# Two-layer decoder on one core: the rotated-heads stage written with small product tiles, and 36 products ahead of its first rows

## The chip, the core and the metric

The kernel runs on one core of one Trainium2 chip, by itself. The time is the device time of one execution in microseconds (us). In the texts PE is TensorE (matrix products), PEld its weight loads, DVE is VectorE, ACT is ScalarE, POOL is GpSimd and SP is SyncE. The engines run their own instruction lists in order and wait for one another on semaphores. Products write to PSUM, which has eight banks.

## What is computed

A decoder of two layers over 32 batch entries of 100 rows and 256 columns in float32. Each layer adds to the rows an attention, a cross-attention to a context and a feed-forward part with experts. The change touches the attention of layer 1 alone ("the rotated heads"), cut here to what matters:

```python
Q = (x @ wq + bq).reshape(Bn, Sn, Hn, hd)     # 16 heads of 16; K and V alike
def prep(t):                                   # for Q and for K
    h1 = jnp.tanh(jnp.einsum('bshd,do->bsho', t, w1) + b1)
    return jnp.einsum('bsho,on->bshn', h1, w2) + b2
q1 = jnp.einsum('bshn,nm->bshm', qc, Hc)       # qc: prep(Q) as 8 complex numbers
qe = jnp.real(jnp.einsum('hcb,bshn->cshn', R, q1))  # R turns entries 0..7 in pairs, else the identity
qq = jnp.sum(qe ** 2, -1)
kk = jnp.sum(ke ** 2, -1)
s = qq[:, :, None, :] * kk[:, None, :, :]
attn = jax.nn.softmax(s / s, axis=2)
out = jnp.einsum('bijh,bjhd->bihd', attn, V).reshape(Bn, Sn, Dn)
return out @ wo + bo
```

Since s / s is 1, the weights are uniform where s is finite and not zero, so each output row is the mean of V over the entry's rows, times a factor of 1 that is still worked out from the squared sizes of every query and of the largest and smallest key of each head.

## The kernel before

The kernel is a chain of stages (self-attention, cross-attention, a mixture stage, the rotated heads, a wide cross-attention, the experts). Each stage is a block of five instruction lists, one for each engine, and the next block begins when all five have ended. The order within a list is the order of the code; no scheduler changes it.

The stage at issue is `rotation_phase` (line 1916). It takes the 32 entries as 16 pairs (`LANES` = 2 entries, 400 columns together: two chunks of 128 of the 256 features, two entries, 100 rows). The entries of pairs 0 to 3 are the *turned* ones (`TURNED` = 4); for pairs 4 to 15 R is the identity. For each pair PE does

- `make_rows` (L2050): four transposes of the normalised rows into the bank `side`;
- `make_part` (L2057), once for K and once for Q: four products of 200 columns into `side`;
- `first_layer` 0 to 7 (L2084): four products of 32 rows and 400 columns, side by side on four row groups of the array, into two of six banks (`BANK_PAIRS` = 3 pairs of banks in turn); ACT takes each bank pair with one tanh (L2210);
- `last_layer` 0 to 3 (L2098): eight products of 32 output rows and 400 columns, side by side on four column groups, into the bank `vec`;
- `make_mean` (L2065): four products of 2 columns into `side`;
- for a turned pair `mix` (L2106, L2108) for K and for Q: one product of 400 columns and two of 200;
- `norms` (L2113) for K and for Q: one product of 128 by 128 on 400 columns, which writes each head's sum of squares to all 16 rows of the head;
- `project` (L2119): four products of 256 columns.

Step k of PE interleaves pair k with the pair before (its query norms and projection) and the pair after (its rows, K, Q and mean). `side` is one bank that all of these share one after another; each user has to wait until DVE or ACT has read what the one before left. ACT copies rows, K and Q out of it (`keep_rows`, `keep_part`), DVE does the rest: `ends_of_keys` (largest and smallest key), `spans`, `weigh` (a reciprocal and three products over 400 columns), `add` (the projection onto x), and also `combine`, `second_norm`, `stats` and `apply`, which end the mixture stage for the pair after next and normalise its rows; POOL gathers rows for `combine` by indirect DMA and works out the roots, the bias and the second norm's scale.

SP waits until the rows of pairs 0 and 1 are stored and then starts the loads of the next stage's weights.

## Time and profile before

| | us |
|---|---|
| median of 3 runs | 3473.21 (3470.78 to 3478.59) |
| the profiled execution | 3493.37, its span 3491.2 |
| the rotated-heads stage in it, from the first product of its tables to its last add | 1228.6 to 1641.0 |
| first rows of the stage reach PE | 1247.1 |
| last product of the stage before, first product of the stage after | 1223.9, 1647.6 |
| PE busy in the span | 3271.7 (94%) |
| DVE, ACT, POOL busy in the span | 1814.3 (52%), 1613.6 (46%), 1520.3 (44%) |
| mean granted TensorE clock, as a share of 2.4 GHz | 0.97 |

The granted clock is at one of two levels, 1.00 (2.4 GHz) or 0.50 (1.2 GHz). In this stage it stands at 0.50 from the first table product until 1268.0 and again from 1633.6 to 1640.0. A timeline row gives start, duration, engine, line, operation, what is written and read, how many instructions are merged into it, and in brackets how long the engine was idle before it and who ended that. A product in float32 shows as two records, so x8 on PE is four products; transposes show as one. Since records overlap, the cost of a group of products is best read as the time from its start to the start of the next group.

### The profile page before, as it was taken

The numbers are of one execution on the slowest core, as the hardware profiler recorded it, in microseconds if no ns is written. First come the engines' busy times: TensorE is split into PE (matmuls) and PEld (weight loads), VectorE is DVE, ScalarE is ACT, GpSimd is POOL, SyncE is SP. The second block draws the span as 40 slices with busy tenths as digits, with TensorE's granted clock in tenths as the row PEclk, the third lists the DMA queues.
The fourth block names the chain that finished last, engine by engine and source line by source line (L and its number), as shares of the span: only waits on it lengthen the run. The fifth ranks groups of instructions, "written<-read, shape, count | busy, mean of one in ns | idle before, by whom it ended". The sixth has DMA issues, their size and how long they took to land. (4 is left out here: it accounts for less than half of the span.)

```text
span 3491.2 us, 70582 instructions
## 1 busy us (share of the span) xinstructions
PE 3271.7 (94%) x26268; PEld 2383.1 (68%) x26269; DVE 1814.3 (52%) x5671; ACT 1613.6 (46%) x3299; POOL 1520.3 (44%) x2061
## 2 busy tenths in 40 slices
PE   8997999988998869998999999999999999999997
PEld 6774566656776734443677777777777688999986
DVE  4665777755887545664444545454545465111123
ACT  4653666655764046775445554555555411111111
POOL 1002444434775154551566566666666554000035
PEclk9999999998998879999999999999999999999998
DMA  8501111100000630001000000000000013999952
GB/s 279 207 2 42 42 42 42 43 26 1 21 23 25 196 90 20 20 20 38 8 8 14 8 8 8 14 8 8 8 14 1 1 38 129 326 326 325 325 185 78
DMA packets 111486, 263.29 MB, mean 75 GB/s; under 512 B 24003, under 2 KB 70240, under 8 KB 95840
## 3 DMA queue, kind: packets, MB, share of 16 engines
q1 hardware_dynamic: 90208, 224.70, 20.1%
q0 software_dynamic: 16384, 26.29, 2.7%
q10 hardware_dynamic: 4608, 8.39, 0.6%
q8 instruction: 191, 3.13, 0.4%
q14 instruction: 95, 0.78, 0.1%
HBM read 196.61 MB, written 62.65 MB: 74 GB/s over the span
## 5 line engine op out<-in xcount | busy, mean ns | idle before, releaser
L2546 POOL TENSOR_SCALAR wide_probs<-wide_probs,wide_inverse 100x361 f32<-100x361 f32 x512 | 603.9, 1192 | 0.1
L2813 ACT ACTIVATE wide_probs<-wide_probs,wide_least 100x361 f32<-100x361 f32 x512 | 300.9, 592 | 8.6 <-DVE wide_least L2910 8.6
L2910 DVE CUSTOM_DVE_ANT_0 wide_probs<-banks,wide_bias 100x361 f32<-100x361 f32 x512 | 251.6, 529 | 45.1 <-issue 40.0
L2598 PE MATMUL banks<-w_wide_v,wide_c 64*120 64x512 f32 (+1 forms) x1152 | 266.4, 591 | 0.9 <-DVE wide_v L2896 0.9
L2592 PE MATMUL banks<-wide_c,w_wide_k 64*128 64x361 f32 x1536 | 257.4, 467 | 7.4 <-DMA wide_c<-in_ctxT 7.4
L2210 ACT ACTIVATE rot_h<-banks,w_rot_b 128x800 f32<-128x800 f32 x256 | 223.6, 924 | 86.2 <-PE banks L2084 81.1
L2544 POOL TENSOR_TENSOR wide_hold_pool<-eps 100x1 f32<-100x1 f32 x256 | 49.4, 193 | 455.1 <-DVE wide_inverse L2916 455.1
L3354 ACT ACTIVATE tiles_hT<-banks 128x512 f32<-128x512 f32 x114 | 68.1, 597 | 347.8 <-PE banks L3270 347.8
L3270 PEld LDWEIGHTS banks<-tiles_xT,tiles_w 128*128 128x128 f32 x1824 | 214.1, 193 | 4.5 <-issue 1.6
L2592 PEld LDWEIGHTS banks<-wide_c,w_wide_k 64*128 64x128 f32 x1536 | 150.5, 189 | 96.6 <-issue 10.5
L2625 PE MATMUL banks<-wide_kT,wide_qT 64*100 64x361 f32 x1024 | 208.4, 478 | 8.3 <-DVE wide_least L2910 6.6
L3270 PE MATMUL banks<-tiles_xT,tiles_w 128*128 128x128 f32 x1824 | 214.6, 276 | 1.2 <-DVE tiles_xT L3516 1.2
L3283 PE MATMUL banks<-tiles_w,tiles_hT 128*128 128x256 f32 x912 | 206.4, 379 | 0.3 <-issue 0.3
L3192 POOL TENSOR_TENSOR combine_hold<-eps 100x1 f32<-100x1 f32 x32 | 7.6, 236 | 442.0 <-DMA slots<-tiles_out 431.9
L2598 PEld LDWEIGHTS banks<-w_wide_v,wide_c 64*120 64x120 f32 (+1 forms) x1152 | 120.7, 180 | 107.1 <-issue 93.3
L3283 PEld LDWEIGHTS banks<-tiles_w,tiles_hT 128*128 128x128 f32 x912 | 168.8, 190 | 21.1 <-issue 0.4
L2643 PEld LDWEIGHTS banks<-ident,wide_probs 100*120 100x120 f32 (+1 forms) x1536 | 142.5, 140 | 31.2 <-issue 29.3
L2643 PE MATMUL banks<-ident,wide_probs 100*120 100x100 f32 (+1 forms) x1536 | 158.8, 254 | 3.0 <-ACT wide_probsT L2819 3.0
L2807 ACT COPY wide_v<-banks 120x512 f32<-120x512 f32 (+1 forms) x96 | 56.2, 585 | 223.7 <-PE banks L2598 223.7
L2804 ACT COPY wide_kT<-banks 128x361 f32<-128x361 f32 x128 | 59.0, 461 | 205.7 <-PE banks L2592 205.7
L2920 DVE COPY wide_probsT<-banks 121x400 f32<-121x400 f32 x128 | 72.9, 570 | 151.2 <-PE banks L2643 151.2
L2655 PE MATMUL banks<-wide_probsT,wide_v 120*64 120x100 f32 (+1 forms) x3072 | 148.9, 253 | 0.1
(469 smaller groups left out, 7378.6 us busy)
## 6 DMA issues: line engine op xcount, KB each, us to landing
tiles_w<-in_moe_w SPq DMA_DIRECT2D x114, 1024.0 KB, 5.1
slots<-zeros SPq DMA_DIRECT2D x58, 512.0 KB, 5.7
cross_c<-in_ctxT SPq DMA_DIRECT2D x32, 270.8 KB, 4.4
wide_c<-in_ctxT SPq DMA_DIRECT2D x32, 270.8 KB, 4.0
mix_kT<-slots SPq DMA_DIRECT2D x32, 256.0 KB, 4.2
slots<-mix_m_tiles_out ACTq DMA_DIRECT2D x32, 256.0 KB, 4.0
tiles_rows<-slots SPq DMA_DIRECT2D x57, 128.0 KB, 4.7
slots<-tiles_out SPq DMA_DIRECT2D x57, 128.0 KB, 4.9
```

The source lines that it names most:

```text
L2210: nc.scalar.activation(t.h[:, u % 2, m, 2 * half:2 * half + 2, :], pair_banks(i), ACT.Tanh, bias=w.b1[:, m:m + 1]).then_inc(h_done[i], 1)
L2546: last = nc.gpsimd.tensor_scalar(t.probs[:, i, j, :], t.probs[:, i, j, :], t.inverse[:, i, j:j + 1], None, ALU.mult)
L2592: last = nc.tensor.matmul(make_bank(unit, lane)[:, 0:CTX], w.k[rows_of(lane), k, at:at + P], t.c[rows_of(lane), of.buf, k, :], start=(k == ...
L2598: last = nc.tensor.matmul(make_bank(unit, lane)[0:kw, :], t.c[rows_of(lane), of.buf, k, k0:k0 + kw], w.v[rows_of(lane), k, of.hf * BANK:(o ...
L2625: last = nc.tensor.matmul(scores(j), t.qT[rows_of(j), here.hf, m, lane, :], t.kT[rows_of(j), here.hf, m, lane, :], start=True, stop=True)
L2643: last = nc.tensor.transpose(turned(bank)[0:cols, at], t.probs[:, i, j, k0:k0 + cols], g.ident[0:S, 0:S])
L2655: last = nc.tensor.matmul(out[rows_of(j), :], t.v[0:kw, of.hf, k, LANE_OF(i), at:at + WD], t.probsT[0:kw, group % STEP_GROUPS, bank, cols] ...
L2813: last = nc.scalar.activation(t.probs[:, i, j, :], t.probs[:, i, j, :], ACT.Exp, bias=t.least[:, i, j:j + 1], scale=-1.0, accum_out=t.rows ...
L2910: last = nc.vector.tensor_tensor_reduce(t.probs[:, i, j, :], scores(j), t.bias[:, :], -1.0, LARGEST, ALU.add, ALU.min, t.least[:, i, j:j + 1])
L2920: nc.vector.tensor_copy(t.probsT[:, group % STEP_GROUPS, 0, :], turned(0)[0:TMAX, 0:TURN_COLS]).then_inc(b[group].probsT_dve, 1)
L3270: last = nc.tensor.matmul(out_, t.w1[:, lane, c, m * P:(m + 1) * P], t.xT[:, lane, c, :], start=(c == 0), stop=(c == DC - 1))
L3283: last = nc.tensor.matmul(tile_out, t.hT[:, lane, m, :], t.w2[:, lane, m, :], start=(m == 0), stop=(m == HM - 1))
```

## The change

The stage is written anew. The products that make up the two layers, the rows, K, Q and the mean are the same in number and shape. Others are cut differently:

- `norms` is four products of 32 output rows and 100 columns, one for each entry and chunk, each on its own column group (`COPIES` = 4 copies of each of 8 heads' sums instead of 16). What follows from them on DVE (`ends_of_keys`, `spans`, `weigh`) runs over 128 by 100 instead of 128 by 400.
- `mix` writes 64 output rows for each chunk, so the two chunks use two column groups; the squares of a turned pair are 200 columns instead of 400.
- The projection is two steps: `make_projected` multiplies the mean, masked by head and copied (`masked`, from DVE), with the projection's weights (four products of 32 output rows and 256 columns on four column groups), DVE copies the result (`keep_projected`), and `project` multiplies the factors with it (two products of 64 rows and 256 columns; for pairs 4 to 15 into two banks, `side` and `vec`; for turned pairs into one, the second waiting for the first through `lane_ready`).
- `keep_rows` and `keep_part` move from ACT to DVE, but for pair 0.
- The mean of a pair is made one step later, next to the rows of another; the order of the groups in a step and of DVE's and POOL's work is new. POOL reads the gather's indices directly, without DVE's copy.
- Between the table products and the first rows PE issues `WARM_UPS` = 36 products of 128 by 128 on 400 columns of the loaded weights into the six banks; nothing reads them.
- ACT runs one tanh of a single column ahead of the first rows.
- On DVE at the stage's head `combine` of pair 1 comes ahead of `apply` of pair 0, and the storing of pair 1's rows moves from POOL to DVE.

```diff
+CHUNK_HEADS = P // HD
+COPIES = 4
+GROUP_ROWS = CHUNK_HEADS * COPIES
+MIXED = CHUNK_HEADS * NQ
+LAST_PAIR = PAIRS - 1
+WARM_UPS = 36
...
+        def norms_in(p, part):
+
+            if is_turned(p):
+                return D, lambda lane, c: t.sum_mixed[:, c * GROUP_ROWS:(c + 1) * GROUP_ROWS], lambda lane, c: mixed_lanes(t.squares[:, part, :])[:, lane, :]
+            return 0, lambda lane, c: t.sum8[:, :], lambda lane, c: by_both(t.squares[:, part, :])[:, c, lane, :]
...
-            def norms(pr, part, ready):
-                pe.wait_ge(squares[part], pr[2])
-                nc.tensor.matmul(side[:, 0:COLS], t.sum8[:, :], t.squares[:, part, :], start=True, stop=True).then_inc(ready, 1)
...
-            def project(pr):
-                pe.wait_ge(s.headsT, pr[2])
...
                 for lane in range(LANES):
                     for c in range(DC):
-                        last = nc.tensor.matmul(by_lane(side)[:, lane, :], t.headsT[:, c, lane, :], w.proj[:, c, :], start=(c == 0), stop=(c == DC - 1))
-                last.then_inc(s.proj_ready, 1)
...
+                for c in range(DC):
+                    nc.tensor.matmul(side[c * MIXED:(c + 1) * MIXED, 0:LANES * S], t.real[:, :], by_chunk(t.by_cos)[:, c, :], start=True, stop=False)
...
+                        last = nc.tensor.matmul(mixed_lanes(side)[c * MIXED:(c + 1) * MIXED, lane, :], t.imag[:, :], by_both(t.by_sin)[:, c, 1 - lane, :], start=False, stop=(lane == LANES - 1))
+                last.then_inc(mixed_ready[part], 1)
+
+            def norms(p, part, out, ready):
+                pe.wait_ge(squares[part], p + 1)
+                _, sums, rows = norms_in(p, part)
+                for lane in range(LANES):
+                    for c in range(DC):
+                        group = lane * DC + c
+                        last = nc.tensor.matmul(out[group * GROUP_ROWS:(group + 1) * GROUP_ROWS, :], sums(lane, c), rows(lane, c), start=True, stop=True)
+                last.then_inc(ready, 1)
+
+            def make_projected(p):
+
+                pe.wait_ge(s.masked, p + 1)
+                for group in range(LANES * DC):
+                    last = nc.tensor.matmul(rows_out[group * GROUP_ROWS:(group + 1) * GROUP_ROWS, :], t.masked[:, group, :, :].rearrange("p h r -> p (h r)"), w.proj[:, group % DC, :], start=True, stop=True)
+                last.then_inc(s.rows_ready, 1)
+
+            def project(p):
+                pe.wait_ge(s.ratio, p + 1)
+                pe.wait_ge(s.rows, p + 1)
+                half = P // LANES
+                if two_banks(p):
+                    for lane, out in ((0, side), (1, vec)):
+                        last = nc.tensor.matmul(out[0:S, 0:D], t.least[lane * half:(lane + 1) * half, :], t.rows[lane * half:(lane + 1) * half, :], start=True, stop=True)
+                    last.then_inc(s.proj_ready, 1)
+                else:
+                    nc.tensor.matmul(by_lane(side)[:, 0, :], t.least[0:half, :], t.rows[0:half, :], start=True, stop=True).then_inc(s.lane_ready, 1)
+                    pe.wait_ge(s.lane_ready, p + 1)
+                    nc.tensor.matmul(by_lane(side)[:, 1, :], t.least[half:P, :], t.rows[half:P, :], start=True, stop=True).then_inc(s.proj_ready, 1)
...
+            def step(k):
+                before, after = k - 1, k + 1
+                late = not two_banks(before)
+                first_layer(k, 2)
+                if before >= 0:
+                    if before > 0:
+                        pe.wait_ge(s.added, before * LANES)
+                    pe.wait_ge(s.k_ends, k)
+                    pe.wait_ge(s.q_kept, k + 1)
+                    make_mean(before)
+                    if is_pair(after):
+                        make_rows(after)
+                first_layer(k, 3)
+                last_layer(k, 0)
+                if before >= 0:
+                    if is_pair(after):
+                        pe.wait_ge(s.yT, after + 1)
+                    pe.wait_ge(s.mean, before + 1)
+                    if is_turned(before):
+                        mix(before, 0)
+                    else:
+                        norms(before, 0, query_norms(before), s.qn_ready)
+                first_layer(k, 4)
+                if before >= 0 and is_pair(after):
+                    if is_turned(before):
+                        pe.wait_ge(squares[0], before + 1)
+                    else:
+                        pe.wait_ge(s.spans, before + 1)
...
+                first_layer(k, 5)
+                last_layer(k, 1)
+                if before >= 0:
+                    if is_pair(after):
...
+                    make_projected(before)
+                    if is_turned(before):
+                        norms(before, 0, query_norms(before), s.qn_ready)
+                first_layer(k, 6)
...
+                elif late:
+                    pe.wait_ge(s.rows, before + 1)
+                    pe.wait_ge(s.spans, before + 1)
                     make_part(after, 0, s.q_ready)
...
+                else:
+                    pe.wait_ge(squares[1], k + 1)
+                    project(before)
+                first_layer(k, 7)
+                last_layer(k, 2)
+                if before < 0:
+                    pe.wait_ge(s.k_kept, after + 1)
+                elif late:
+                    pe.wait_ge(s.q_kept, after + 1)
+                else:
+                    pe.wait_ge(s.added, (before + 1) * LANES)
+                if is_turned(k):
+                    mix(k, 1)
+                else:
+                    norms(k, 1, key_norms, s.kn_ready)
...
+                        pe.wait_ge(s.k_ends, k + 1)
+                    if before >= 0 and late:
+                        project(before)
+                    else:
+                        make_part(after, 0, s.q_ready)
+                    first_layer(after, 1)
...
-            make_rows(FIRST)
-            pe.wait_ge(s.yT, 1)
-            make_part(FIRST, 1, s.k_ready)
-            pe.wait_ge(s.k_kept, 1)
-            make_part(FIRST, 0, s.q_ready)
...
+            for k in range(WARM_UPS):
+                nc.tensor.matmul(pair_banks(k)[:, 0, :], w.qkv[:, 0, 0:P], w.qkv[:, 1, 0:COLS], start=True, stop=True)
+            make_rows(0)
+            make_part(0, 1, s.k_ready)
+            first_layer(0, 0)
+            make_part(0, 0, s.q_ready)
+            first_layer(0, 1)
...
+            nc.scalar.activation(t.warm[:, :], w.b1[:, 0:1], ACT.Tanh)
...
-            def keep_rows(pr):
-                act.wait_ge(s.yT_ready, pr[2])
-                nc.scalar.copy(t.yT[:, :, :, :], by_both(side)).then_inc(s.yT, 1)
...
+                    combine(following)
+                if is_pair(after):
+                    keep_rows(after)
+                if before >= 0:
+                    keep_mean(before)
+                if is_pair(after):
+                    add_rows_up(after)
+                if before >= 0 and not is_turned(before):
                     spans(before)
-                if after:
-                    apply(after)
-                if before:
                     weigh(before)
-                if following:
+                if before < 0:
                     combine(following)
-                if after:
-                    add_rows_up(after)
-                if third:
-                    copy_slots(third)
-                if following:
+                    turn_by(k, 1)
```

PE, the last half of a step in the middle of the stage, pairs that are not turned, in the kernel before:

```order
L2084 MATMUL banks<-rot_q,rot_w 128x400 x4
L2119 MATMUL banks<-w_rot_proj,rot_headsT 100x256 x4
L2098 MATMUL banks<-rot_h,rot_w 32x400 x8
L2084 MATMUL banks<-rot_q,rot_w 128x400 x4
L2065 MATMUL banks<-rot_ybar,w_rot_qkv 128x2 x4
L2084 MATMUL banks<-rot_q,rot_w 128x400 x4
L2113 MATMUL banks<-rot_squares,rot_sum 128x400
L2098 MATMUL banks<-rot_h,rot_w 32x400 x8
L2084 MATMUL banks<-rot_q,rot_w 128x400 x4
L2113 MATMUL banks<-rot_squares,rot_sum 128x400
L2084 MATMUL banks<-rot_q,rot_w 128x400 x4
```

The projection and both norms in a step of the changed kernel (L2079 is `first_layer`, L2095 `last_layer`, L2052 `make_part`, L2060 `make_mean`, L2116 `norms`, L2123 `make_projected`, L2132 `project`):

```order
L2116 MATMUL banks<-rot_squares,rot_sum 32x100 x4
L2079 MATMUL banks<-rot_q,rot_w 128x400 x4
L2052 MATMUL banks<-rot_yT,w_rot_qkv 128x200 x4
L2079 MATMUL banks<-rot_q,rot_w 128x400 x4
L2095 MATMUL banks<-rot_h,rot_w 32x400 x8
L2123 MATMUL banks<-w_rot_proj,rot_masked 32x256 x4
L2079 MATMUL banks<-rot_q,rot_w 128x400 x4
L2132 MATMUL banks<-rot_rows,rot_least 100x256 x2
L2079 MATMUL banks<-rot_q,rot_w 128x400 x4
L2095 MATMUL banks<-rot_h,rot_w 32x400 x8
L2116 MATMUL banks<-rot_squares,rot_sum 32x100 x4
```

Two single products of 400 columns have become fours of 100 columns, the projection's four products have become four narrow ones and two; between the two first_layer groups around `project` only that short group is left, where before a last_layer or `make_mean` stood.

PE at the head of the stage in the changed kernel, from the tables to the first layer of pair 0:

```order
L2031 MATMUL banks<-w_rot_hadamard,w_rot_w2T 128x32 x4
L2033 MATMUL banks<-ones,w_rot_v_b 128x1 x2
L2035 MATMUL banks<-w_rot_b,rot_fold_b 128x1
L2228 MATMUL banks<-w_rot_qkv 128x400 x36
L2044 MATMUL banks<-ident,rot_y 128x100 x4
L2052 MATMUL banks<-rot_yT,w_rot_qkv 128x200 x4
L2079 MATMUL banks<-rot_q,rot_w 128x400 x4
L2052 MATMUL banks<-rot_yT,w_rot_qkv 128x200 x4
```

The 36 products stand ahead of the transposes of pair 0 in the same list, so those can't begin before all 36 have been issued.

DVE, one step of the changed kernel from the copy of the rows on:

```order
L2385 COPY rot_yT<-banks 128x400
L2393 SCALAR_TENSOR_TENSOR rot_mean<-banks,rot_v_b 128x2x2
L2397 TENSOR_TENSOR rot_masked<-rot_mean,own_scaled 128x128
L2389 TENSOR_REDUCE rot_ybar<-rot_yT 128x4
L2429 TENSOR_SCALAR rot_least<-banks,rot_k_least 128x100
L2430 TENSOR_SCALAR rot_most<-banks,rot_k_most 128x100
L2436 RECIPROCAL rot_inverse<-rot_least 128x100
L2438 TENSOR_TENSOR rot_least<-rot_least,rot_inverse 128x100
L2440 SCALAR_TENSOR_TENSOR rot_least<-rot_most,rot_least 128x100
L2403 TENSOR_SCALAR rot_q<-banks,w_rot_qk_b 128x200 x2
```

The two copies, of rows and of K, now stand in DVE's list among the short operations of the pair before, right behind `combine` of the pair after next.

## Rows read from the trace of the kernel before

**Rows 1.** Windows of the stage: us, busy per engine (instructions), PE clock, DMA share.

```profile
1233.00:1247.10 14.10, 0.00 (x0) 0.00 (x0) 7.53 (x27) 0.00 (x0) 9.11 (x16) 0.50 0.18 50
1247.10:1268.10 21.00, 17.28 (x72) 10.12 (x76) 7.14 (x21) 10.24 (x14) 13.62 (x22) 0.50 0.49 142
...
1286.70:1367.50 80.80, 73.90 (x544) 36.12 (x540) 46.94 (x110) 49.87 (x69) 38.87 (x66) 1.00 0.06 16
1367.50:1392.20 24.70, 23.07 (x182) 11.07 (x178) 14.62 (x36) 16.71 (x23) 11.44 (x21) 1.00 0.04 10
1392.20:1611.40 219.20, 214.40 (x1683) 100.33 (x1680) 131.89 (x306) 168.23 (x230) 117.45 (x202) 1.00 0.07 18
1611.40:1629.00 17.60, 15.15 (x128) 5.47 (x124) 7.24 (x10) 11.55 (x14) 0.00 (x0) 1.00 0.00 1
1629.00:1641.00 12.00, 4.65 (x14) 2.44 (x10) 6.18 (x8) 0.59 (x1) 0.00 (x0) 0.72 0.00 0
1647.60:1653.60 6.00, 5.99 (x20) 3.83 (x22) 1.34 (x2) 0.46 (x1) 1.77 (x3) 0.50 1.05 368
```

**Rows 2.** Timeline of PE, one step of pairs that are not turned.

```profile
1440.39 0.53 PE L2050 MATMUL banks<-ident,rot_y 100*128 100x100 f32 x4
...
1441.73 1.62 PE L2057 MATMUL banks<-rot_yT,w_rot_qkv 128*128 128x200 f32 x8
...
1448.09 0.95 PE L2084 MATMUL banks<-rot_q,rot_w 32*128 32x400 f32 x8
1449.07 1.97 PE L2119 MATMUL banks<-w_rot_proj,rot_headsT 128*100 128x256 f32 x8
1450.97 1.55 PE L2098 MATMUL banks<-rot_h,rot_w 128*32 128x400 f32 x16
1452.45 0.95 PE L2084 MATMUL banks<-rot_q,rot_w 32*128 32x400 f32 x8
1453.34 1.05 PE L2065 MATMUL banks<-rot_ybar,w_rot_qkv 128*128 128x2 f32 x8
1454.52 0.95 PE L2084 MATMUL banks<-rot_q,rot_w 32*128 32x400 f32 x8
1455.40 0.94 PE L2113 MATMUL banks<-rot_squares,rot_sum 128*128 128x400 f32 x2
1456.27 1.55 PE L2098 MATMUL banks<-rot_h,rot_w 128*32 128x400 f32 x16
```

**Rows 3.** Timeline of PE, the mixes and the norms of a turned pair.

```profile
1362.87 0.94 PE L2106 MATMUL banks<-rot_by_cos,rot_real 128*128 128x400 f32 x2
1363.65 0.84 PE L2108 MATMUL banks<-rot_by_sin,rot_imag 128*128 128x200 f32 x4
1365.16 0.94 PE L2113 MATMUL banks<-rot_squares,rot_sum 128*128 128x400 f32 x2 [0.67 <-ACT rot_squares L2215]
...
1369.34 0.91 PE L2106 MATMUL banks<-rot_by_cos,rot_real 128*128 128x400 f32 x2 [0.88 <-DVE rot_by_sin L2337]
```

**Rows 4.** Timeline of PE, the mixture stage: narrow products of 100 columns, side by side.

```profile
901.06 0.88 PE L750 MATMUL banks<-mix_probsT,mix_v 100*17 100x100 f32 x32
```

**Rows 5.** Timeline of PE, the expert stage: a dense stream of products of 256 columns.

```profile
2959.77 3.62 PE L3283 MATMUL banks<-tiles_w,tiles_hT 128*128 128x256 f32 x16
2963.22 3.73 PE L3270 MATMUL banks<-tiles_xT,tiles_w 128*128 128x128 f32 x32
```

**Rows 6.** Timeline of PE, step 15: a first_layer group that waits for the tanh.

```profile
1617.92 0.95 PE L2084 MATMUL banks<-rot_q,rot_w 32*128 32x400 f32 x8 [1.11 <-ACT rot_h L2210]
```

**Rows 7.** Timeline of DVE: combine of one pair until its next work, and the last reciprocal.

```profile
1444.55 0.87 DVE L2304 SCALAR_TENSOR_TENSOR rot_moe_sum<-rot_moe_got,mix_coef,mix_x 100x256 f32<-100x256 f32 x2
...
1447.20 0.54 DVE L2325 TENSOR_REDUCE rot_ybar<-rot_yT 128x4 f32<-128x400 f32 x1
...
1631.88 2.65 DVE L2357 RECIPROCAL rot_inverse<-rot_least 128x400 f32<-128x400 f32 x1
```

556 lines of the change are left out of this document (277 added, 279 removed).

## The prediction

> **What bounds the kernel now.** I read the page first: PE is busy for 94% of the span, and the stages follow one another without overlap, so the stage that is changed can be costed alone. Its windows [rows 1] say the same of the stage. Between 1392.2 and 1611.4, which is steps 5 to 14 (pairs that are not turned), PE is busy for 214.4 of 219.2 us, ACT for 168, DVE for 132: PE is the bound, at 21.92 us a step. Steps 1 to 3 (1286.7 to 1367.5) take 26.93 us each, step 4 24.7, step 15 17.6. The tail after the last last_layer takes 12.0. At the head PE does nothing from 1233 to 1247.1; then it works at half clock for 21 us, and step 0 ends at 1286.7, 39.6 us after the first rows.
>
> **What a product costs.** Eight products of 256 columns take 3.45 us from start to start [rows 5], 1.69 ns a column, so 400 columns are 0.675. The lone norms group takes 0.87, first_layer (four side by side) 0.88, last_layer (two rounds of four) 1.48 against 1.35 [rows 2]: a group costs its columns plus 0.13 to 0.2 us. Four products on four column groups cost one. This holds for narrow short ones too: sixteen of 100 columns took 0.88 us [rows 4], which is four rounds of 0.17 plus 0.2. So I price a group as 1.69 ns times the columns of its rounds, plus 0.2.
>
> Those 32 records took 28 ns each. The Trainium skill, "TensorE: Matmul & The Clock Gate", "Part 2: What happens when you issue a matmul", has about 62 ns for each product where the sequencer's firmware decodes it. By that the 32 records would take 2.0 us and the eight of a new norms group 0.5 instead of 0.37, some 5 us more over the stage; the row speaks for the lower price.
>
> **Norms and projection, pairs not turned.** A norms group goes from 0.87 to 0.17 + 0.2 = 0.37, twice a step: -1.0. The bounds are 0.22 (the quarter of [rows 4]) and 0.87 (no overlap). The projection goes from 1.90 (from 1449.07 to 1450.97 [rows 2]) to two groups of one round of 256 columns, 0.43 + 0.2 each: 1.26, -0.64. Bounds: 0.9 and 2.5 (four rounds and one). PE's list for such a step is then 8 first_layer at 0.88, 4 last_layer at 1.48, two parts at 1.55, rows 0.46, mean 1.18, norms 0.74, projection 1.26: 19.7 us, where the same sum was 21.4 before, 0.5 below the measured step.
>
> **What is late next.** The three bank pairs tie first_layer to the tanh: in step 15 a group that had only the tanh to wait for started 0.95 + 1.11 = 2.06 us after the one before [rows 6]. Around `project` the new distance is 0.88 + 0.63 = 1.51, so PE waits 0.55 there; from group 7 to the next pair's group 0 both its tanh must have ended (2.06 and another 0.8), some 2.8, and there are 0.88 + 1.48 + 0.37 = 2.73, another 0.1. Step: 20.3, a gain of 1.6 on 21.92, for ten steps **-16**. What hides the rest: the step has eleven handovers of `side`, and each has at least one first_layer (0.88) as cover. On DVE an operation on 400 columns is about 0.57, so the short ones on 100 are 0.2, the copies of K and Q 0.6, the copy of the projection 0.4, the reciprocal (2.65 for 400 columns [rows 7]) 0.7. The longest chain runs from the key norms to the next rows: ends 0.5, stats 1.0, roots on POOL 1.7, apply 0.8, combine 2.65 (1444.55 to 1447.20 [rows 7]), copy of the rows 0.6, semaphores 0.5: 7.8, against 0.88 + 1.55 + 0.88 + 1.48 + 0.88 + 1.18 + 0.46 + 0.88 + 1.48 = 9.7 on PE. Slack 1.9; if the chain is longer, each step pays the rest. ACT loses 2.2 us a step and has room.
>
> **Turned pairs.** Two mixes were 0.78 + 0.71 each and two waits of 0.67 for the squares and one of 0.88 for the turning stood open [rows 3]. Now a mix is 200 + 2 x 100 columns in rounds of two, 0.68 + 0.2 = 0.88, and squares and turning have a first_layer and more between. PE's list is 19.7 + 2 x 0.88, plus 0.6 because `project` does its two products one after the other: 22.1. DVE at the step's start does ends, turning, combine, rows and mean, 0.5 + 1.2 + 2.65 + 0.6 + 0.4, behind the key norms; PE reaches the mix about 0.5 us earlier than that: 22.7. Against 26.93 that is -4.2 three times, **-12.7**; step 4 has one mix less, 22.0 against 24.7, **-2.6**. Bounds for the three: 21.8 (no gap, mixes at 0.7) and 24.5.
>
> **Step 15 and tail.** Step 15 gets a second mean (1.2) and three tanh-bound distances of 2.06 against less norms: **+0.3**. In the tail the chain was norms, spans 1.1, reciprocal 2.65, three products 1.8, a projection at half clock, adds 0.8: 12.0. Now masked projection 0.6, copy 0.5, norms 0.4, spans 0.5, reciprocal and two products 1.3, project 0.7 at full clock since no idle time is long, adds 0.8 and handovers: 5.2. **-6.8**.
>
> **The head.** The 36 products start at 1233. At full clock each is 0.675 to 0.72, 0.69 taken; at half clock 1.35. In the dense start of the next stage 6.0 us passed at 0.50, the last window of [rows 1]; I take 5 here. Then 3.7 products run in them and 32.3 follow in 22.3: the end is at 1260.3, with bounds 1257 and 1262. The first rows, with combine of pair 1 now ahead of them, are ready at about 1250, so the stage starts 13.2 us later than at 1247.1. Against that, at full clock the head and step 0 go through in 27.1 instead of 39.6: rows 0.5, copy 0.6, K 1.55 and its copy 0.9, then groups at the tanh's distance, to 1287.4 against 1286.7. **+0.7**; the clock pays for the products and no more. The one tanh on ACT takes a table load out of the way; it is in the 27.1. The moved combine and stores of pair 1 on DVE are hidden behind the 36 products, and the next stage's loads start some 2 us earlier, with nobody waiting for them here.
>
> **Sum.** 0.7 - 12.7 - 2.6 - 16 + 0.3 - 6.8 = -37.1. The profiled span goes from 3491.2 to 3454. The profiled execution was 20 us above the median; as the saving lies in counted work I take it off the median: 3473.2 - 37 = **3436**.
>
> **The rivals.**
> - *DVE comes first.* The chain of 7.8 us is longer than 9.7, because POOL and DVE slow each other or a handover has no cover. At 1 us a step it costs 15: gain 22, 3451. For it: DVE gets four copies and sits in front of nearly every use of `side`. Against: it was busy for 60% of the stage and loses more than it gets. 0.19.
> - *More than I think.* Groups at 0.22 and 0.5, no wait for the tanh, the 36 products over by 1257: another 10 us, 3426. 0.09.
> - *The small tiles don't run side by side.* Norms stay at 0.87, the masked projection costs 1.9, the mix 1.5: the step is 22.4, turned ones 26.3, and the tail keeps 5 us; the sum is about +1: 3474. This would be the change not doing what it says. [Rows 4] speaks against it. 0.05.
> - *The clock falls inside the stage (slower).* At half clock a step's 19.7 of products take about 36, so each costs 16.5 more; from 2.3 such steps on the kernel is slower, and with three 12 us slower: 3486. At the head PE was busy for 17.3 of 21.0 us with much the same groups and stayed at 0.50 [rows 1], so less dense work might not hold the level. Against it: steps at 91% busy kept 1.00 [rows 1]. The Trainium skill, "TensorE: Matmul & The Clock Gate", "A second HAM failure mode: psum-queue depth-cycling", says that short idle times between groups can be enough to make the clock go up and down. 0.05.
>
> **The numbers.** The forecast (gain 29 to 45) has 0.62. A measurement of this kernel tells about 0.2%, 7 us, from no change. Faster: 0.62 + 0.19 + 0.09 = 0.90; same 0.05; slower 0.05. Bounds of the ten steps (+10, -4), of the turned ones (+5, -3), and of the head (+2, -3) and the first rival's 3451 with some more give the range 3421 to 3457.
>
> **What would show it.** In the changed profile: norms groups at 0.37 and no wider; first_layer behind `project` waiting 0.5 for ACT; steps of 20.3 and 22.7; PE waiting for DVE nowhere but before the mix; rows at 1260 at clock 1.00; 5 us from the last last_layer to the last add. Wrong would be steps above 21, a clock of 0.50 behind the 36 products, or waits for the copies of rows or K.

## The result, and the profile after

| | before | after |
|---|---|---|
| time, us, median (lowest to highest) | 3471.99 (3469.98 to 3478.59) | 3428.3 (3424.14 to 3429.3) |
| ratio, with its 95% interval | | 0.9869 (0.9852 to 0.9886) |
| profiled execution, and its span | 3493.37, 3491.2 | 3428.55, 3426.7 |
| the stage: first table product to the next stage's first product | 419.0 | 378.9 |
| the span from there to its end | 1843.6 | 1820.2 |

The predicted 3436 us was 8 us above the time, and the range of 3421 to 3457 holds it. The change takes 43.7 us off the median. The two spans differ by 64.5 us, of which 40.1 lie in the stage, 23.4 behind it and 0.9 ahead of it, in code that the change does not touch. The runs below show what the 23.4 go with.

The windows of after (us; busy time of PE, PEld, DVE, ACT and POOL, with instructions; granted clock of PE; DMA share and GB/s). The first holds the 36 products, the next three are cut where steps begin, as in [rows 1]; the fifth has the length of steps 5 to 14 and is cut at the rows, 1.8 us behind the start of step 5 (1380.4):

```profile
1232.10:1258.70 26.60, 26.58 (x72) 14.82 (x73) 12.68 (x41) 0.86 (x2) 14.48 (x22) 0.91 0.34 111
1258.70:1286.10 27.40, 23.11 (x197) 11.47 (x195) 8.88 (x25) 19.30 (x26) 12.62 (x20) 1.00 0.68 144
1286.10:1315.10 29.00, 24.47 (x212) 12.12 (x212) 15.80 (x49) 14.49 (x19) 16.78 (x29) 0.88 0.05 15
1315.10:1358.80 43.70, 42.66 (x420) 21.46 (x416) 26.05 (x80) 29.35 (x37) 25.50 (x41) 1.00 0.08 20
1382.20:1579.40 197.20, 190.05 (x1842) 91.47 (x1841) 111.72 (x338) 149.42 (x181) 112.02 (x176) 1.00 0.07 18
1579.40:1594.60 15.20, 12.92 (x142) 5.49 (x145) 4.37 (x14) 10.15 (x13) 0.00 (x0) 1.00 0.01 2
1594.60:1600.00 5.40, 1.86 (x24) 0.57 (x16) 3.03 (x8) 0.59 (x1) 0.00 (x0) 0.88 0.00 0
```

Row by row these are the 36 products; the head and step 0; step 1; steps 2 and 3; ten steps' length, 19.72 each; the last 15 us of step 15; the tail. Ten steps took 219.2 us before. Step 1 stands out: steps 2 and 3 take 21.8 each, it takes 29.0, and its clock is 0.88, which is a part of it at 0.50.

| term of the sum | predicted | measured |
|---|---|---|
| head and step 0 | +0.7 | +0.3 |
| step 1 (22.7 predicted, 26.9 before) | -4.2 | +2.1 (29.0) |
| steps 2 and 3 | -8.5 | -10.2 (21.8 each) |
| step 4 | -2.6 | -3.1 |
| steps 5 to 14 | -16 | -22 (19.72 each) |
| step 15 | +0.3 | -0.4 |
| tail, from the end of the last last_layer (1594.8) to the end of the last add (1599.9) | -6.8 | -6.9 (5.1) |
| sum | -37.1 | -40.2 |

**One step of the pairs that are not turned**, PE's timeline of after, to be held against [rows 2]:

```profile
1402.38 0.95 PE L2079 MATMUL banks<-rot_q,rot_w 32*128 32x400 f32 x8
1403.27 1.55 PE L2095 MATMUL banks<-rot_h,rot_w 128*32 128x400 f32 x16
1404.63 0.35 PE L2116 MATMUL banks<-rot_squares,rot_sum 128*32 128x100 f32 x8
1404.92 0.95 PE L2079 MATMUL banks<-rot_q,rot_w 32*128 32x400 f32 x8
...
1409.61 0.61 PE L2123 MATMUL banks<-w_rot_proj,rot_masked 128*32 128x256 f32 x8
1410.15 0.95 PE L2079 MATMUL banks<-rot_q,rot_w 32*128 32x400 f32 x8
1411.03 0.68 PE L2132 MATMUL banks<-rot_rows,rot_least 64*100 64x256 f32 x4
1412.21 0.95 PE L2079 MATMUL banks<-rot_q,rot_w 32*128 32x400 f32 x8 [0.50 <-ACT rot_h L2255]
...
1414.46 0.35 PE L2116 MATMUL banks<-rot_squares,rot_sum 128*32 128x100 f32 x8
1415.03 0.95 PE L2079 MATMUL banks<-rot_q,rot_w 32*128 32x400 f32 x8 [0.22 <-issue]
```

From start to start, the norms (L2116) take 0.29 us, the masked projection (L2123) 0.54, and `project` (L2132) 0.68 and a wait of 0.50 for the tanh. All three were in the prediction, at 0.37, 0.63 and 0.63 with a wait of 0.55. The second norms group is followed by a gap of 0.22 us more.

**Step 1**, three engines of after: PE, DVE, then POOL.

```profile
1289.37 0.38 PE L2116 MATMUL banks<-rot_squares,rot_sum_mixed 128*32 128x100 f32 x8 [3.19 <-DVE rot_q L2403]
1289.68 0.95 PE L2079 MATMUL banks<-rot_q,rot_w 32*128 32x400 f32 x8
1291.69 1.65 PE L2060 MATMUL banks<-rot_ybar,w_rot_qkv 128*128 128x2 f32 x7 [1.05 <-DVE rot_k_least L2424]
```

```profile
1278.90 0.73 DVE L101 TENSOR_SCALAR rot_moe_sum<-rot_moe_sum,rot_ln_meanvar,rot_ln_rstd 100x256 f32<-100x256 f32 x2
1287.63 0.75 DVE L85 BATCH_NORM_STATS2 rot_ln_stats<-x 100x6 f32<-100x256 f32 x2 [8.01 <-POOL x L1995]
...
1288.59 0.73 DVE L2403 TENSOR_SCALAR rot_q<-banks,w_rot_qk_b 128x200 f32<-128x200 f32 x2
```

```profile
1276.59 0.19 POOL L94 TENSOR_TENSOR rot_ln_vareps<-rot_ln_meanvar,eps 100x1 f32<-100x1 f32 x1 [10.62 <-DVE rot_ln_meanvar L89]
...
1278.40 1.07 POOL L1979 DMA_INDIRECT rot_moe_got<-slots,mix_slot_i  x1 [0.20 <-issue]
...
1283.45 1.42 POOL L1989 TENSOR_TENSOR rot_moe_sum<-rot_moe_sum,w_mix_ln_w 100x256 f32<-100x256 f32 x2
1284.82 1.42 POOL L1992 TENSOR_TENSOR rot_moe_sum<-rot_moe_sum,w_mix_ln_b 100x256 f32<-100x256 f32 x2
1286.20 1.39 POOL L1995 TENSOR_TENSOR x<-x,rot_moe_sum 100x256 f32<-100x256 f32 x2
```

Read from the end: PE waits 3.19 us for DVE's copy of Q(1). The copy stands in DVE's order behind the statistics of rows(2), which wait 8.01 us for POOL's last add. POOL's last three operations on these rows, of which that add is the third (4.2 us), stand behind four gathers of rows(3) (1278.40 to 1283.45), and these behind square roots for which POOL had waited, doing nothing, for 10.62 us. In the kernel before, the gather stood behind these three; the change has put it ahead of them.

The clock adds its part. Behind the two waits it stood at 0.50 for 6.8 us:

```profile
1291.50:1298.30 6.80, 6.61 (x36) 3.44 (x36) 5.08 (x16) 2.66 (x4) 3.14 (x6) 0.50 0.01 2
```

The four groups in it (mean, rows, first_layer, last_layer) took 6.85 us from start to start, where the same groups at full clock take 3.75. So of the 7.2 us that step 1 takes more than step 2, some 3.1 are the lower clock and the rest are the waits of 3.19 and 1.05.

### The profile page after: what moved, and what is told of

Same layout as the page of the kernel before. It is cut to its first block and busy times, and to the rows that moved or that the text cites. A ratio compares the mean times of both kernels' runs of the same rounds, so it can differ in the third digit from the quotient of the medians.

```text
span 3426.7 us, 71349 instructions
## 1 busy us (share of the span) xinstructions
PE 3240.3 (95%) x26644; PEld 2373.2 (69%) x26645; DVE 1784.2 (52%) x5737; ACT 1585.8 (46%) x3225; POOL 1516.5 (44%) x2022
## 5 line engine op out<-in xcount | busy, mean ns | idle before, releaser
L2713 PEld LDWEIGHTS banks<-wide_kT,wide_qT 64*100 64x100 f32 x1024 | 85.3, 163 | 89.8 <-issue 42.5
```

What stands on the lines that cost most here:

```text
L2713: last = nc.tensor.matmul(scores(j), t.qT[rows_of(j), here.hf, m, lane, :], t.kT[rows_of(j), here.hf, m, lane, :], start=True, stop=True)
```

## The experiments

Three groups of four, each group on one chip. The length of the stage, read from each trace as above, compares kernels better than the time of the whole program, whose executions spread by some 10 us; the ratios alone can't tell most of the changed kernels from one another, since their intervals overlap.

| run | stage, us | first table product to first rows | rows(0) to rows(2) | ratio to before (95%) |
|---|---|---|---|---|
| before | 419.0 | 18.5 | 46.8 | 1 |
| before, second profile | 419.0 | 18.6 | 46.5 | |
| before with 20 products | 418.8 | 20.4 | 44.8 | 1.0005 (0.9994 to 1.0017) |
| before with 36 products | 427.7 | 30.4 | 43.8 | 1.0032 (1.0020 to 1.0044) |
| after | 378.9 | 31.1 | 34.7 | 0.9869 (0.9852 to 0.9886) |
| after, again | 379.1 | 31.3 | 34.6 | 0.9882 (0.9867 to 0.9898) |
| no products | 372.5 | 20.5 | 36.0 | 0.9878 (0.9861 to 0.9895) |
| 20 products | 370.1 | 20.3 | 34.7 | 0.9856 (0.9833 to 0.9878) |
| early gather | 375.4 | 30.7 | 29.9 | 0.9882 (0.9864 to 0.9900) |
| no products, early gather | 365.2 | 20.4 | 33.7 | 0.9848 (0.9833 to 0.9863) |
| 20 products, early gather | 361.6 | 20.5 | 29.9 | 0.9827 (0.9813 to 0.9840) |

Rows(0) to rows(2) is the time from PE's first transpose of pair 0 to its first of pair 2; it holds the head, step 0 and the start of step 1. The four kernels of the first group ("no products", "20 products", "early gather" and "before with 36 products") ran on a chip on which the changed kernel's steps of turned pairs are longer: from rows to rows 22.5 us instead of 21.8 twice, then 21.95 instead of 21.3, and the ten steps together 0.4 more. That makes 2.4 us of the stage of a changed kernel, and 3.1 with the early gather, where the stretch ahead of these shows it too (22.77 to 22.09). On like chips "no products" is thus 8.8 us shorter than after, "20 products" 11.2, "early gather" 6.6. These three are estimates, since after itself has no run on that chip; two kernels of the last group, which differ from after in steps 5 to 14 alone, show the same 22.5, 22.5 and 21.95 to within 0.04. The stage of before is 419.0 us in both profiles.

### The products taken away, or fewer of them

```diff
-WARM_UPS = 36
+WARM_UPS = 0
```

> The changed kernel without the 36 products ahead of the first rows; everything else as changed. What is tested is what the 36 products bring. Clock theory (they hold the clock up, and cost a wait of 10.7 us, since in the trace of after the rows were ready at 1248.0 and PE took them at 1258.73): without them rows(0) begin at about the same moment as in the kernel before (10.7 us earlier), but head and step 0 go at the granted clock 0.50 as there. With narrow tiles the head's products at half the clock cost about twice their 27 us of busy time, so the loss is 8 to 15 us and the sum is between -3 and +5 us against after: 3425 to 3433 us, ratio to before 0.9865 to 0.989. Rival (the clock isn't bought by the products, it would have come up anyway): 10.7 us less, 3418 us, ratio 0.9845. Second rival (without them the clock stays low into steps 1 and 2): over 3440 us.

```diff
-WARM_UPS = 36
+WARM_UPS = 20
```

> The changed kernel with 20 products ahead of the first rows instead of 36: they end at about 1247.8 on the times of after, as the rows come (1248.0). Theory (16 of the 36 are too many: they stand ahead of work that is ready): the head begins 10.7 us earlier at the full clock, step 0 too; all engines behind follow, so -10.7 us, 3418 us, ratio to before 0.9845. Rival (DVE and POOL bound steps 0 and 1: their combines, norms and gathers aren't moved by TensorE's start): only a part comes back, -4 to -7 us, 3421 to 3424 us, and the waits of TensorE in step 1 grow by what is missing. Second rival (20 products aren't enough to hold the clock): as without products, 0 to +5 us.

The windows from rows(0) to rows(2), without products and then with 20:

```profile
1245.00:1281.00 36.00, 27.53 (x221) 14.64 (x221) 16.14 (x47) 21.43 (x28) 21.42 (x34) 0.93 0.69 171
```

```profile
1244.84:1279.55 34.71, 26.26 (x220) 13.72 (x221) 16.62 (x48) 21.43 (x28) 21.49 (x34) 0.96 0.75 177
```

Without products the rows start 10.5 us earlier and the stretch behind them takes 1.3 us longer. The granted clock stood at 0.50 until about 1249.6, under 5 us behind the first rows, and then rose to 1.00 by itself; in both kernels it fell once more for 6.8 us in step 1, as in after. The stage is 6.4 us shorter than that of after, 8.8 on like chips. By the stage the clock theory fell and the first rival (10.7) is the nearest: the 36 products do not give back what they cost. The ratio does not say so: 0.9878 lies in the range that the theory gave (0.9865 to 0.989), and its interval is as wide as 12 us. With 20 products they cost nothing, since they end as the rows come: 8.8 us shorter as measured, 11.2 on like chips, where 10.7 was expected.

### The gather ahead of the roots, in step 0 alone

```diff
             for k in range(PAIRS):
+                if k == 0:
+                    gather(3)
                 if is_pair(k + 2):
                     roots(m0, k + 2)
-                if is_pair(k + 3):
+                if k > 0 and is_pair(k + 3):
                     gather(k + 3)
```

> The changed kernel; at step 0 alone POOL issues the gather of rows(3) ahead of its square roots for combine(2) instead of behind them. Step 1 took 29.0 us where its neighbours take 21.8, with waits of TensorE for DVE's keep of Q (3.19 us) and key minimum (1.05 us), and a granted clock of 0.50 for some 6 us behind them. Theory (POOL's 5.2 us of gather stand between the roots and the add of rows(2), DVE's statistics wait 8.01 us for that, and Q(1) is queued behind them; POOL was idle from 1266 to 1276.6): with the gather in the idle time the statistics wait some 3 us, the keep of Q comes 5 us earlier, the clock doesn't fall: step 1 takes 22 to 23 us, in all -5.5 to -7 us, 3422 us, ratio to before 0.9855. Rival (DVE is what is late, since combine(2) stands behind keep_rows(1), POOL is only where its wait shows): step 1 stays at 27 to 29 us, 3426 to 3429 us.

POOL and DVE of this kernel:

```profile
1262.45 1.07 POOL L1979 DMA_INDIRECT rot_moe_got<-slots,mix_slot_i  x1 [0.20 <-issue]
...
1275.66 1.52 POOL L1989 TENSOR_TENSOR rot_moe_sum<-rot_moe_sum,w_mix_ln_w 100x256 f32<-100x256 f32 x2 [1.16 <-DVE rot_moe_sum L101]
```

```profile
1279.96 0.75 DVE L85 BATCH_NORM_STATS2 rot_ln_stats<-x 100x6 f32<-100x256 f32 x2 [4.05 <-POOL x L1995]
```

The gather now lies in POOL's idle time, the adds follow the roots at once, DVE waits 4.05 us instead of 8.01, and PE's wait of 3.19 is gone. From rows(1) to rows(4) the kernel takes 61.8 us, after 66.9: -5.2, though two of the three stretches in it are 0.68 us longer on this chip each. Of the stage it makes 6.6 us on like chips. From rows(0) to rows(2) it is 29.9 against 34.7. The clock stays at 1.00. By the stage the theory holds in mechanism and size. The ratio was expected at 0.9855 and came at 0.9882 (0.9864 to 0.9900): on this chip the changed kernel's turned pairs are longer, which the expectation did not have.

### The products alone, in the kernel before

```diff
+            for k in range(36):
+                nc.tensor.matmul(pair_banks(k)[:, 0, :], w.qkv[:, 0, 0:P], w.qkv[:, 1, 0:COLS], start=True, stop=True)
             make_rows(FIRST)
```

> The kernel before with nothing but the same 36 products ahead of its first rows: the products without the small tiles. Theory (in the sum of the prediction the head came out at +0.7: the products delay the rows by about 11 us and the clock gives about that back): 0 +/- 2 us against before, 3470 to 3474, ratio 0.9995 to 1.0005. Rival (the products are worth something by themselves, since the wide tiles at half the clock cost more than 11 us): -3 to -8 us, ratio 0.998 to 0.999. Second rival (the delay is kept and the clock gives less): +3 to +10 us.

The stage takes 427.7 us, 8.7 more, and the ratio agrees. The first two pairs, at full clock at first, gain only 3.0 us on the 46.8, and the clock falls to 0.50 once more, behind 1264, in the old head:

```profile
1258.00:1262.00 4.00, 3.17 (x22) 2.04 (x20) 0.00 (x0) 1.94 (x5) 4.00 (x7) 1.00 0.00 0
...
1266.00:1270.00 4.00, 2.26 (x12) 1.09 (x16) 0.83 (x2) 2.93 (x4) 2.56 (x5) 0.50 1.01 382
```

It is the second rival. With 20 (the same line with `range(20)`):

> The kernel before with 20 of the products instead of 36, which end before its first rows are there (18.5 us behind the first table product). With 36 it was 1.0032 of before, the stage 427.7 us instead of 419.0: 11.9 us of delay, 3.0 back in the head, and the clock fell to 0.50 once more at 1264 in the old order of the head. Theory (what products bring is that the head runs at the full clock, and that is 3 us in the old order, 4 in the new one; the delay is what costs): stage 415 to 417 us, ratio 0.999. Rival (20 products end too early to hold the clock, or the old order of the head loses it anyway): 419, ratio 1.000. Rival (at the full clock throughout, the head gives the 11 us of the prediction): 408, ratio 0.997.

Here the 20 products end behind the moment at which the old kernel's rows are ready, not ahead of it as I had thought: rows come 1.8 us later, 1.7 to 2.1 come back, the clock falls near 1256. The stage is 418.8, the ratio 1.0005. That is the first rival. In the old order the products bring nothing at any number tried.

### The kernel before once more

> The kernel before, as it is: a second profile of it. In the first one the granted clock stayed at 0.50 for 21 us behind the first rows, and the last stage was some 23 us longer than in the profile of after. If the slow clock of the head is how this order of work behaves: again 0.50 for 15 us or more, rows of pair 1 21 to 22 us behind the first. If it is chance, since the changed kernel without products rose after 4 us in one profile and after 10 in another: anything from 4 to 21 us. The stage should be 417 to 419 us, and the rest of the span 1820 to 1825 us if the last stage's 23 us were a disturbance of that one execution.

The stage takes 419.0 us again. The clock behind the first rows stayed at 0.50 for about 10 us, rose, fell at 1257 and rose again, where in the first profile it stayed down for 21 us; the stretch to rows(2) took 46.5 and 46.8 us all the same. So when the clock rises is not fixed, and the shorter time at 0.50 gave the old head 0.3 us. The rest of the span took 1839.7 us, not the 1820 to 1825 that I expected. Over all traces the rest is 1843 to 1848 us in the four of the first group (this code and the changed one alike), 1839 to 1841 in the four of the last, and 1817 to 1824 in the four of the middle. The 23.4 us between the profiles of before and after (1843.6 and 1820.2) therefore go with the chip, or with what else the runs of a group had in common, and not with the change. On which chip those two were taken is not on record.

### After again, and both edits together

> The changed kernel as it is, on the same chip and in the same rounds as the next two, so that the length of the stage and the whole time can be set side by side. The stage is counted from the first table product to the next stage's first product: 378.9 us in the trace of after, 419.0 before. If the stage depends on the kernel alone: 378 to 380. Rival (the chip of the first four runs gives longer turned steps: there rows came 22.5 us apart in steps 2 and 3, here 21.8): 380 to 381 on such a chip.

The stage takes 379.1 us, as first measured. Steps 2 and 3 take 21.8 us here too, so this run does not put the rival to the test. The time is 3427.66 against 3467.99 of before on the same chip, which is 40.3 us for 40 us of stage.

> 20 products instead of 36, and at step 0 the gather of rows(3) ahead of the roots: both edits at once. Apart they gave stages of 370.1 (20 products) and 375.4 (gather). Theory (two separate causes, 16 superfluous products ahead of ready rows, and one misplaced gather): the savings add up, the stage takes 364 to 366 us, 13 to 16 us under the unchanged one beside it; ratio to before 0.9845 or less. Rival (with the earlier start the gather's place no longer decides, since POOL and DVE aren't moved by TensorE's start): 369 to 370.

> No products, and the gather early. Without products the head went from half clock to the full one by itself 4 us after the first rows, in one profile. Theory (that is how this order of the head behaves, the products are not needed): the stage takes 366 to 368 us, 2 us more than with 20 products. Rival (the early rise was a chance of that execution; the head at half clock costs 10 us): 374 to 378.

The second and third windows of the kernel with 20 products (rows(0) to rows(2), rows(2) to rows(3)), then that of the kernel without (rows(0) to rows(2)):

```profile
1249.36:1279.24 29.88, 25.13 (x222) 12.97 (x221) 15.82 (x46) 21.01 (x28) 21.48 (x34) 1.00 0.84 206
1279.24:1301.33 22.09, 21.30 (x210) 10.73 (x210) 13.28 (x42) 14.11 (x18) 12.70 (x20) 1.00 0.08 20
```

```profile
1246.66:1280.34 33.68, 28.91 (x220) 15.83 (x221) 15.81 (x46) 21.14 (x28) 21.49 (x34) 0.86 0.75 183
```

With both edits the stage takes 361.6 us, 17.5 less than after beside it, and the time is 3409.56 against 3427.66, 18.1 less. The savings apart, on like chips, add up to 17.8, so the causes are separate, as the theory has it (my 364 to 366 left out what the chip had added to both). The clock never falls. It is the best version: 0.9827 of before. Without products the stage is 365.2, 1 us under the range of the theory and 3.6 over the kernel with 20, where 2 were expected; the clock stood at 0.50 for about 10 us behind the first rows and not for 4, and the stretch to rows(2) takes 3.8 us more than with 20. The rival (374 to 378) fell. So the products are worth 1.3 to 3.8 us here, as long as they delay nothing.

### What a norms group costs

```diff
+                times = 2 if 5 <= p <= 8 else 4 if 10 <= p <= 13 else 1
-                for lane in range(LANES):
-                    for c in range(DC):
+                for lane, c in [(lane, c) for _ in range(times) for lane in range(LANES) for c in range(DC)]:
```

> The changed kernel; the norms groups of pairs 5 to 8 are issued twice and those of pairs 10 to 13 four times (the same result again), two groups a step; the other steps stand beside them in the same trace at 19.7 us. It measures what a group of four narrow products costs, and how much of TensorE's time shows in the step. Theory (TensorE's list is the bound, four such products run side by side in 100 columns, 0.17 us): each repeat adds 0.17, steps of pairs 5 to 8 +0.34 (20.1), of 10 to 13 +1.0 (20.7). Rival (the products don't run side by side, 0.17 each): +1.4 and +4.1. Second rival (the steps wait for the tanh, and a repeat is taken from the wait): +0 and +0.5.

The steps are 19.72 us unchanged, 19.89 with each group twice, 20.47 with each four times: +0.17 and +0.75. One group, four times, and the next of PE:

```profile
1493.79 0.87 PE L2116 MATMUL banks<-rot_squares,rot_sum 128*32 128x100 f32 x32
1494.59 0.95 PE L2079 MATMUL banks<-rot_q,rot_w 32*128 32x400 f32 x8
```

Three more sets of four products take 0.80 - 0.29 = 0.51 us, 0.17 a set: the four run side by side. Of the two groups in a step one shows in full and the other fills the gap of 0.28 first: 0.17 + 0 and 0.51 + (0.51 - 0.28) = 0.74, as measured. The price of 0.17 is that of the theory, but the step grew by less than it said (0.34 and 1.0) and by more than the second rival said (0 and 0.5), since neither had the gap. TensorE's list is the bound but for such gaps.

### DVE made slower

```diff
                 if not is_turned(k):
                     ends_of_keys(k)
+                for i in range(2 if 5 <= k <= 8 else 5 if 10 <= k <= 13 else 0):
+                    nc.vector.reduce_sum(t.pad[:, i, :].rearrange("p (c l) -> p c l", l=LANES), t.yT[:, :, :, :], AX.X)
```

> The changed kernel with extra reductions on DVE that nothing reads (0.56 us each), right behind the ends of the key norms: two more in each of steps 5 to 8 (+1.1 us), five more in steps 10 to 13 (+2.8 us); the steps between stand beside them at 19.72. It measures how far DVE is from being the bound. Theory (the prediction's slack of 1.9 us on the chain from the key norms to the next rows): steps 5 to 8 stay at 19.7, steps 10 to 13 go to 20.6. Rival (DVE stands directly behind TensorE at every handover of the shared bank): +1.1 and +2.8. Second rival (the slack is larger than I made it): both stay within 0.2 of 19.72.

Steps with 1.1 us more take 20.0 us, with 2.8 us more 20.93, beside 19.74. In the latter PE waits at two places:

```profile
1505.32 0.38 PE L2116 MATMUL banks<-rot_squares,rot_sum 128*32 128x100 f32 x8 [0.48 <-DVE rot_yT L2385]
...
1512.81 0.68 PE L2132 MATMUL banks<-rot_rows,rot_least 64*100 64x256 f32 x4 [0.98 <-DVE rot_rows L2411]
```

Of 1.1 us more 0.26 shows, of 2.8 us 1.2, so DVE hides 0.9 of the one and 1.6 of the other, against the 1.9 of the prediction: no case of three as stated, the theory the nearest. DVE is close behind.

### Two parts undone: one bank for the projection, and K on ACT

```diff
-                if two_banks(p):
+                if two_banks(p) and not 5 <= p <= 8:
                     for lane, out in ((0, side), (1, vec)):
...
                 tanh(k, 4)
+                if 10 <= k <= 13:
+                    keep_part(1, s.k_ready, s.k_kept, after)
                 tanh(k, 5)
```

> The changed kernel with two parts undone, each in four steps, the others beside them at 19.72. Pairs 5 to 8 (steps 6 to 9): the projection's two products go one behind the other into one bank, as for the turned pairs (1.33 us in the trace of after instead of 0.68, where TensorE then waits 0.50 for the tanh). In steps 10 to 13 the copy of K is on ACT between two tanh instead of on DVE. Theory (TensorE's list and its waits for the tanh fill the step): the serial projection eats the wait of 0.50 first and shows 0.15 to 0.25 of its 0.65, so 19.9 us; the copy of K (0.75 on ACT) pushes the tanh behind it and all after it in the step, of which TensorE has about 0.7 of waits to give: +0.4 to +0.8, so 20.1 to 20.5. Rival (TensorE's list alone): +0.65 and 0. Rival (ACT has room, as its busy share of 78% says): +0.2 and 0.

PE with one bank, and ACT with the copy of K:

```profile
1409.39 0.66 PE L2135 MATMUL banks<-rot_rows,rot_least 64*100 64x256 f32 x2
1410.10 0.67 PE L2137 MATMUL banks<-rot_rows,rot_least 64*100 64x256 f32 x2
1410.71 0.95 PE L2079 MATMUL banks<-rot_q,rot_w 32*128 32x400 f32 x8
```

```profile
1486.34 0.74 ACT L2268 ACTIVATE rot_q<-banks,w_rot_qk_b 128x200 f32<-128x200 f32 x2 [0.43 <-PE banks L2052]
1487.11 1.75 ACT L2255 ACTIVATE rot_h<-banks,w_rot_b 128x800 f32<-128x800 f32 x2
```

The serial projection takes 1.32 us, its wait for the tanh is gone, and the step is 19.97 to 20.01 us: +0.25, as the theory had it. The second bank is thus worth 2.5 us over ten steps. With K's copy on ACT the steps stay at 19.76 to 19.77, +0.0. There the theory fell, and the rival that ACT has room is right: the copy went into the time in which ACT waits for PE, and in these steps moving it to DVE earns nothing by itself.

## Why the prediction was right, point by point

**What bounds the stage.** Shown: repeating 0.17 us of narrow products lengthens the step by 0.17 where no gap is behind them.

**Norms and projection.** The mechanism is right and the size a little short: steps of 19.72 instead of 20.3. The term that was mis-sized is PE's list. The norms took 0.29 (0.37 taken), the masked projection 0.54 (0.63), the mean 0.91 (1.18 kept from [rows 2]), and last_layer in front of a narrow group 1.36, where it keeps 1.48 in front of first_layer. That is -0.16, -0.09, -0.27 and -0.36 a step, -0.9 in all, against which the waits and `project` are 0.2 over mine: -0.7, where 0.6 were missing. The Trainium skill, "TensorEngine Tiling (Array Packing)", "Key Properties", says that a change of tiling mode drains TensorE. The rows agree in kind: last_layer and the norms both use column groups of 32, first_layer does not, and 0.12 us is the difference. No run isolated it, and why the mean took 0.91 instead of 1.18 is open.

**The lower price of short products.** [Rows 4] gave 0.37 us for a group and was right to go by: 32 records went in 0.80 us, 25 ns each, and the group came even below 0.37. The Trainium skill, "TensorE: Matmul & The Clock Gate", "Part 2: What happens when you issue a matmul", has 62 ns for each product where the sequencer's firmware decodes it. By that the estimate for a group was 0.5 us; no trace here shows that price.

**What is late next.** The wait of 0.55 behind `project` was 0.50, and the one-bank run shows it as such, since 0.64 us of work in its place cost 0.25. The chain on DVE had 1.9 us of slack in the prediction; the padded run shows 0.9 to 1.6, so that term was taken too large, at no cost here.

**Turned pairs.** Steps 2 and 3 took 21.8 where I had 22.7; the wait at the mix is 0.23 instead of 0.5. On the chips of the first and last group these steps take 22.5: there PE waits 0.90 us for the copy of the projected rows, where it had a gap of 0.23 on the other. The steps of the old kernel did not move (26.93 on all). Why the copy comes later there is open.

**Step 1.** This is the one term that failed. I gave it the steady price of 22.7, and it took 29.0. The rival "DVE comes first" was true for this step and no other, not because the chain is long but because POOL's queue held four gathers in front of an add on which DVE and so PE waited. The rival on the clock came true here too, for 6.8 us: it fell behind the waits, and that is some 3.1 of the 7.2 us. The early gather takes both away. The order could have been read before, as the change moves the gather from behind the adds to ahead of them, and steps 0 and 1 are where nothing has run ahead yet. That the total came out within 8 us all the same is partly luck: the 6.3 us missing here were made up by the narrow groups, whose steps 5 to 14 gave 6 us more than counted.

**The head.** +0.7 was predicted and +0.3 measured, and both terms of it were as counted: a delay of 12.5 us for 13.2, and 27.4 us for 27.1 from the first rows to the end of step 0, where the kernel before took 39.6. What is wrong is the reason. I wrote that "the clock pays for the products and no more". Of the delay 2.0 us are rows that are ready later, since DVE does more ahead of them, and 10.5 are products. But without any products the same stretch took 30.7 and 31.1 us (the two kernels with none), so the clock gives under 4 us of the 12.2, and by the stretch to rows(2) 1.3 to 3.8. The other 8.5 us and more came with the clock at 0.50 at first: they are the rest of the rewriting. Its order in the head (first_layer follows K instead of waiting for Q too), its narrow groups and the order of DVE's work act there together, and no run separates them. So the sum came out right while the clock was credited with a gain that it did not make, and the 36 products, which looked free, cost the change an estimated 11 us against 20 products and 9 against none.

**The tail.** 5.1 for 5.2. The reciprocal and the last projection of after:

```profile
1596.81 0.78 DVE L2436 RECIPROCAL rot_inverse<-rot_least 128x100 f32<-128x100 f32 x1
```

```profile
1598.28 0.84 PE L2132 MATMUL banks<-rot_rows,rot_least 64*100 64x256 f32 x4 [2.13 <-issue]
```

The reciprocal takes 0.78 us instead of the 2.65 of [rows 7], as counted. One thing was mis-seen: "full clock since no idle time is long". PE's wait of 2.13 ahead of `project` was followed by a lower clock (0.88 over the tail's window above), so `project` took 0.84 instead of 0.68.

**The base.** Taking the saving off the median and not off the profiled time was right: the profiled execution of before had a rest of the span that was 20 us longer, and so has every kernel on such a chip.

## What to carry to other kernels

Price a repeated step by TensorE's groups, from start to start, and add the waits that stay: that came within 3% here for the steps that are not turned, and within 4% for steps 2 and 3. Price the first one or two repetitions apart, by walking each engine's queue in order, because work issued ahead (here gathers on POOL) can stand in front of the one thing that everybody waits for. Products that only hold the clock up must end when the real ones are ready; before believing in them, take them away in the new order of work, since a faster order and a faster clock show as the same shorter time.

## What the runs showed of the hardware

- The clock's rise is not the same from run to run. Behind the first rows, without products, it stood at 0.50 for about 21 and 10 us in two profiles of the kernel before, and for about 5 and 10 in two of the changed order. In the old head, with gaps of 0.8 to 1.2 us between groups, it fell back from 1.00 to 0.50 in three of three profiles that had reached it early. In the new head, whose gaps are 0.6 to 1.1 us, it stayed at 1.00 in all. It fell in step 1 in or behind PE's wait of 3.19 us and another of 1.05, and behind waits of 1.4, 1.68 and 1.06 in the kernels with 20 products and with none; with the early gather it did not fall. Why the old head loses it is open. The next stage's loads start there too (DMA share 1.01 where it had fallen), but they are not the cause alone: they ran at a share of 0.84 in the fastest kernel, at clock 1.00.
- The groups of runs, each on its own chip, differ in two places: in the rest of the program (1817 to 1824 us in one, 1839 to 1848 in the two others), and by about 0.67 us in each stretch of turned pairs of the changed kernel. The steps 5 to 14 agree to 0.05 us in the changed kernel and to 0.1 in the one before.
- Products of 100 columns on four column groups went at 25 ns a record, sets of four at 0.17 us each.
